# Attention scores as 32-row fp32r products in four row quarters, one ring of six PSUM banks for the scores and the feed-forward, and twice the low halves on GpSimd

## What is computed

```python
x = x + attn(layernorm(x))        # 16 heads of 8 columns, T = 512
#   qkv = x @ w_qkv + b_qkv
#   attn = softmax(where(causal, q @ k.T / sqrt(8), -inf)) @ v
#   out  = attn @ w_proj + b_proj
x = x + ffn(layernorm(x))         # d = 128, 8 experts, hidden 512
#   weights = p * (p > 0.5),  p = sigmoid(x @ Wg + bg)
#   h = relu(x @ W1[e] + b1[e]);  sum over e of weights[e] * (h @ W2[e] + b2[e])
```

## Time and profile before

| | |
|---|---|
| median of 3 runs | 763.07 us (762.34 to 765.86) |
| profiled execution, its own time | 762.58 us |
| its span | 760.8 us |
| PE / DVE / ACT / POOL busy | 723.6 / 528.3 / 407.4 / 276.2 us |
| mean granted clock of PE | 0.982 of full speed |
| PE's idle time before matmuls, from 106 us to 640 us | 534 us less 528.8 us busy |

### The profile page before, as it was taken

One profiled execution on the slowest core, in us unless ns is written; L12 is line 12 of the kernel. 1 busy time (PEld: TensorE's weight loads), 2 busy tenths in 40 slices (PEclk: granted clock), 3 DMA queues, 4 the chain that ended last, 5 costly groups with the idle time before them and its releaser, 6 DMA issues.

```text
span 760.8 us, 13160 instructions
## 1 busy us (share of the span) xinstructions
PE 723.6 (95%) x4515; PEld 413.8 (54%) x4515; DVE 528.3 (69%) x1044; ACT 407.4 (54%) x745; POOL 276.2 (36%) x424
## 2 busy tenths in 40 slices
PE   2969999999999999999999999999999999999996
PEld 2323345566555655555555645556455655567764
DVE  7977787678666786668865687666766676537543
ACT  1355665546555565556555655556545565654442
POOL 4173243334333343235422443333323433333232
PEclk9959999999999999999999999999999999999998
DMA  5521113110231122110221112111221101200300
GB/s 173 146 59 48 48 39 92 53 52 15 56 84 44 37 67 66 51 37 16 67 78 52 26 35 86 45 44 25 66 65 52 38 2 36 65 28 2 96 28 15
DMA packets 37698, 40.63 MB, mean 53 GB/s; under 512 B 5920, under 2 KB 26280, under 8 KB 37632
## 3 DMA queue, kind: packets, MB, share of 16 engines
q1 hardware_dynamic: 37104, 39.60, 18.9%
q10 hardware_dynamic: 528, 0.20, 0.2%
HBM read 23.52 MB, written 2.23 MB: 34 GB/s over the span
## 4 chain that ended last, share of the span: by engine, by line
PE 87%; DVE 4%; SPq 3%; issue 2%; ACT 2%; POOL 1%; DMA 0%; POOLq 0%; DVEq 0%; ACTq 0%
PE pv_bank L1160 11%; PE y_bank L1211 10%; PE z_bank L1026 10%; PE z_bank L1028 8%; PE y_bank L1215 8%; PE z_bank L1027 8%; PE y_bank L1213 8%; PE ring L1085 6%; PE ring L1082 6%; PE ring L1032 5%; PE ring L1098 5%; SPq L567 3%; PE ring L1139 1%; PE ring L1175 1%; PE ring L1026 1%
## 5 line engine op out<-in xcount | busy, mean ns | idle before, releaser
L794 ACT ACTIVATE h_hi<-z_bank 128x512 fp32r<-128x512 f32 x256 | 153.3, 599 | 186.3 <-PE z_bank L1028 159.9
L991 DVE SCALAR_TENSOR_TENSOR h_lo<-z_bank,h_hi 128x512 fp32r<-128x512 f32 x224 | 153.5, 686 | 86.7 <-ACT h_hi L794 85.4
L763 ACT ACTIVATE pt<-ring 128x512 f32<-128x512 f32 x292 | 163.9, 598 | 54.0 <-PE ring L1085 53.8
L941 DVE TENSOR_REDUCE negmax<-ring 128x1 f32<-128x512 f32 (+1 forms) x173 | 115.7, 683 | 43.3 <-PE ring L1098 43.1
L682 POOL TENSOR_SCALAR_AFFINE_SELECT pt<-pt 128x512 f32<-128x512 f32 x128 | 81.0, 645 | 153.5 <-ACT pt L763 153.2
L1211 PE MATMUL y_bank<-h_hi,w_lo 128*128 128x512 f32 x256 | 118.5, 463 | 2.4 <-POOL h_lo L689 1.8
L1026 PE MATMUL z_bank<-x2T_lo,w_hi 128*128 128x512 f32 x256 | 112.6, 440 | 0.2
L699 POOL TENSOR_TENSOR f_buf<-f_buf 128x512 f32<-128x512 f32 x56 | 71.9, 1284 | 107.9 <-DVE f_buf L1002 107.8
L1215 PE MATMUL y_bank<-h_lo,w_hi 128*128 128x512 f32 x256 | 101.1, 395 | 0.0
L1028 PE MATMUL z_bank<-x2T_hi,w_hi 128*128 128x512 f32 x256 | 101.0, 395 | 0.0
L1213 PE MATMUL y_bank<-h_hi,w_hi 128*128 128x512 f32 x256 | 100.6, 393 | 0.0
(11 more groups left out here) (171 smaller groups left out, 835.2 us busy)
## 6 DMA issues: line engine op xcount, KB each, us to landing
f_buf<-gates SPq DMA_DIRECT2D x64, 256.0 KB, 3.3
stack<-parts SPq DMA_DIRECT2D x192, 64.0 KB, 2.1
x_in<-in_L_attn_x SPq DMA_DIRECT2D x8, 256.0 KB, 3.1
pt<-in_L_ffn_W SPq DMA_DIRECT2D x1, 2048.0 KB, 10.0
out_x<-f_buf SPq DMA_DIRECT2D x8, 256.0 KB, 2.4
stack<-stack SPq DMA_DIRECT2D x32, 32.0 KB, 1.9
stack<-nmT SPq DMA_DIRECT2D x64, 6.0 KB
wqkv_in<-in_L_attn_w_qkv ACTq DMA_DIRECT2D x1, 192.0 KB, 3.2
```

What stands on the lines that cost most here:

```text
L763: sc.activation(pt[:, slot, :], b[:], ACT.Exp, scale=SCALE).then_inc(free_sem("ex", i, g, u), 1)
L794: sc.activation(h_hi[:, (i * SLOTS + s) % 3, :], z_bank[s % 2][:], ACT.Relu).then_inc(s_hhi, 1)
L941: v.tensor_reduce(dst, src, AX.X, ALU.max, negate=True).then_inc(free_sem("max", i, g, u), 1)
L991: v.scalar_tensor_tensor(out=h_lo[:, (i * SLOTS + s) % 3, :], in0=z_bank[s % 2][:], scalar=0.0, in1=h_hi[:, (i * SLOTS + s) % 3, :].bitcas ...
```

## The change

The scores' operands become two fp32r halves instead of three bf16 parts: three products of 8 rows and the maximum in two rows fit in 32 rows. Groups 0 and 2 lie in the upper 64 partitions, groups 1 and 3 in the lower 64, a head in a quarter. A call of both kinds, for two groups of different parity, then addresses all four quarters, and its matmuls are issued across the units, first pieces first. Part 1 and part 2 and their instructions go; SP makes 4 transfers for a group instead of 7, and one instead of two for the maxima. `nm` splits in two halves; its transposition becomes four fp32r matmuls with a stationary operand of 128 columns, of which 8 are filled. `z` takes a bank of the common ring, which has six instead of four. 8 of 32 low halves go through POOL, with a single `h_all`. The planner gets other costs, starts a ready `pv` ahead of a call of scores, and delays by two due units (`HALF_DUE`) a call that isn't of both kinds.

```diff
-Q_PART = (0, 0, 1, 0, 1, 2)
-K_PART = (0, 1, 0, 2, 1, 0)
-STACK_DMAS = 7
+Q_PART = (0, 0, 1)
+K_PART = (0, 1, 0)
+STACK_DMAS = 4
...
-RING = 4
-EARLY_RING = RING + 3
+RING = 6
+EARLY_RING = RING + 1
...
-POOL_SPLITS = [s for s in range(SLOTS) if s % 8 == 7]
+POOL_SPLITS = [s for s in range(SLOTS) if s % 4 == 3]
...
             due += SWITCH_DUE if form != "full" else 0
             if best is None or due < best[0]:
                 best = (due, key)
+        if pv and best and pv[0] + (PV_DUE if form == "full" else 0) < best[0]:
+            best = pv
+        if not best:
+            best = pv
         if pairs and free >= 2:
+            due = min(p[0] for p in pairs.values()) + (SWITCH_DUE if form == "full" else 0)
+            if free < 4 or len(pairs) == 1:
+                due += HALF_DUE
             if best is None or due < best[0]:
+                if pv and form == "full":
+                    start(now, "pe", pv[1])
+                    return
...
-        parts = sb("parts", [P, 6, T], BF16)
-        stack = sb("stack", [P, PAIRS, 2, T], BF16)
+        parts = sb("parts", [P, 4, T], F32R)
+        stack = sb("stack", [P, GROUPS // 2, 2, 2, T], F32R)
...
                 elif kind == "stack":
+                    rows = stack[64 * (g % 2):64 * (g % 2) + 64, g // 2].bitcast(F32)
                     for s, (a, b) in enumerate(zip(Q_PART, K_PART)):
+                        sp.dma_start(rows[s::4, :, :, :],
+                                     parts[32 * g:32 * g + 32, a:3 + b:2 + b - a, :].bitcast(F32)
+                                     ).then_inc(s_stack[g], 16)
...
-                elif kind in ("qpart", "kpart"):
-                    pool.wait_ge(*emptied(kind[0], i))
-                    g_.tensor_copy(parts[:, 3 * qk + 1, :], rest[:, qk, :]).then_inc(s_part1, 1)
...
+            def head_rows(g, j):
+                r = 64 * (g % 2) + 32 * (j % 2)
+                return stack[r:r + 32, g // 2, j // 2]
...
+                units = [(False, unit, max_pieces(unit, next_bank("max", *unit))) for unit in mx]
+                units += [(True, unit, exp_pieces(unit, next_bank("ex", *unit))) for unit in ex]
+                for k in range(2):
+                    for last_form, unit, pieces in units:
+                        if k >= len(pieces):
+                            continue
+                        out_, lhsT, rhs = pieces[k]
+                        stop = last_form and k == len(pieces) - 1
+                        last = mm(out_, lhsT, rhs, start=(k == 0), stop=stop, skip_group_check=True)
...
+                    for t in range(TB):
+                        last = mm(b[:, t * P:(t + 1) * P], nm[:, t, :], ident32[:], start=True, stop=True)
+                    last.then_inc(done, 1)
```

More of the change, by code:

```diff
@@ L61 @@
 PER_UNIT = SLOTS / UNITS_PER_SEQ
-SWITCH = 100
+UNIT_COST = 230
+ENTER = {"full": 190, "mask": 92, "scores": 190, "pv": 98}
 SWITCH_DUE = 0.3
-AFTER_PE, AFTER_OTHERS, AFTER_DMA = 170, 70, 2000
+PV_DUE = 0.3
+HALF_DUE = 2
+AFTER_PE, AFTER_OTHERS, AFTER_DMA = 175, 85, 2000
 def work_items():
@@ L239, in list_schedule @@
     emptier = {}
-    mode = "rows128"
+    form = "full"
     def at(time, what, key):
@@ L254, in start @@
     def start(now, engine, key):
-        nonlocal mode, banks
+        nonlocal form, banks
         cost = work[key][1]
@@ L260, in start @@
         if engine == "pe":
[L261 to L264, removed]
+            new = "pv" if item[0] == "pv" else "full"
+            if form != new:
+                cost += ENTER[new]
+            form = new
+            if item[0] not in ("y", "pv"):
                 fill(item)
@@ L273, in start_scores @@
     def start_scores(now, mx, ex):
[L274 to L285, removed]
+        nonlocal form
+        cost = ENTER["scores"] if form != "scores" else 0
+        form = "scores"
+        for unit in (*mx, *ex):
+            fill(unit)
+            ready["pe"].remove(("pe", unit))
+        cost += UNIT_COST * (2 if mx and ex and (mx[0][2] - ex[0][2]) % 2 == 0 else 1)
+        for unit in ex:
+            at(now + cost + AFTER_PE, "done", ("pe", unit))
         if mx:
-            mode = "rows128"
-            cost += SWITCH
+            form = "full"
+            cost += ENTER["mask"]
             for unit in mx:
-                cost += 80
+                cost += UNIT_COST // (4 if unit[3] < GH else 2)
                 at(now + cost + AFTER_PE, "done", ("pe", unit))
@@ L308, in pick_pe @@
                 continue
-            if item[0] not in ("z", "y", "pv") and not free:
+            if item[0] == "pv":
+                if pv is None or due < pv[0]:
+                    pv = (due, key)
+                continue
+            if item[0] != "y" and not free:
                 continue
@@ L443, in block_program @@
         pv_bank = bank("pv_bank")
-        z_bank = [bank("z_bank0"), bank("z_bank1")]
         y_bank = bank("y_bank")
-        ring += [*z_bank, y_bank]
+        ring.append(y_bank)
         s_ident = sem("s_ident")
@@ L1042, in max_pieces @@
                     for j in heads:
-                        rows = stack[64 * (j % 2):64 * (j % 2) + 64, (g * GH + j) // 2]
+                        rows = head_rows(g, j)
                         n = (q + 1) * P
@@ L1106, in _ @@
                     continue
-                if kind in ("z", "y", "pv"):
-                    pass
-                else:
+                if kind not in ("y", "pv"):
                     b = next_bank(*w)
```

199 lines of the change are left out of this document (87 added, 112 removed).

## The result

| | before | after |
|---|---|---|
| median of 4 runs each | 763.12 us (762.34 to 765.86) | 751.89 us (751.27 to 753.44) |
| profiled execution, its own time and its span | 762.58 us, 760.8 us | 752.44 us, 750.7 us |
| mean granted clock of PE | 0.982 | 0.960 |
| first z issued at | 108.12 us | 120.16 us |
| from the first z to the end | 652.7 us | 630.5 us |

The ratio is 0.985 (0.982 to 0.9879): 11 us faster, where 40 were forecast, and just outside the range of 700 to 750. The last two rows split it. From the first z on the kernel gained 22.2 us, with 32.6 forecast (terms 1, 2 and 4). Ahead of it, it lost 12.0 with 7 gained in the forecast: 19 of the missing 29 us. The same items lie ahead of the first z in both, but for one pair of ex units more in the changed kernel.

A forecast was written before the change was run, and what follows sets the result against it. PE was taken to bound the kernel from 106 to 640 us, the start to wait for data. 762.6 us with -35.6 - 3 - 7 + 2 + 4 = -39.6 gave 723 us, range 700 to 750.

The forecast's parts named there:

- Term 1: Calls of scores after the first z: joint calls stream in four quarters, 112.5 us instead of 148, so -35.6 us.
- Term 2: nm's transposition and pv on PE: nm between -6 and +6, taken as 0; pv ahead of calls -3 us.
- Term 4: New waits: y behind POOL's low halves +2 us (up to +26), four banks and common ring +4 (0 to +10).
- What bounds the kernel: PE bounds from 106 to 640 us, DVE has room up to 1.4; before that the start waits for data.
- I take 105 of 126: Number of calls after the first z that become joint, between 60 and 126; those ends give -10 and -47 us.
- pv's -3: A ready pv started ahead of a call of scores saves a border where it stood alone: -3 us, -9 at most.
- The +6: New waits after the first z: +2 us for y behind POOL, +4 for banks and the common ring.
- Term 3, the start: Ahead of the first z: fewer gather transfers and earlier last parts, partly given back by DVE: -7 us (0 to -12).
- The transfers: First sequence's gather on SP: 16 transfers instead of 28, 0.65 us each, so 7.8 us less.
- The calls ahead of the first z: Calls of scores before 106 us get cheaper, but PE waits for data there, so counted as 0.
- its own range: Whole time without rivals, 704 to 740 us, from joint calls (-47 to -25), start (0 to -12), waits (+3 to +14).

The follow-up runs named there:

- six early banks: The changed kernel, but y's bank not lent to the common ring before the first z (six banks there instead of seven): 748.85 us, ratio 0.9724.

## Why the prediction was off

**What bounds the kernel** was right from the first z on. PE sets the end, DVE has room, and PE's idle time didn't grow. For the start it was read from 20 to 60 us alone; from 60 to 108 us PE was busy for 44.97 of 48 us already before the change, and there it is PE's work and clock that count.

**Term 1, the mechanism: right.** The calls in the timeline above, and 786.4 us without joint calls, show that quarters stream together. The Trainium skill ("TensorE: Matmul & The Clock Gate", Part 3) says that row tiles overlap; the trace agrees, eight matmuls of 256 columns from 414.03 to 414.47.

**Term 1, the size: -26 instead of -35.6.** After the first z the planner's order has 81 calls in four quarters and 13 that share a half, where I took 105; 32 of max alone (21) and 38 of ex alone (29). Prices measured there: 0.77, 0.94, 0.73 (0.70 to 0.71 with units of one matmul, mostly 0.77 with two) and 0.63. Together 81 x 0.77 + 13 x 0.94 + 32 x 0.73 + 38 x 0.63 = 122 us, against 112.5 forecast and 148 before. The counts carry most of it: my 105, 21 and 29 at the measured prices make 114.5. The step that failed in this term is "I take 105 of 126". It had bounds (60 to 126), but no reading of when four banks are free and of which half the due groups are.

**Term 2.** nm went from 0.52 to 0.45, 32 times: -2 instead of 0. pv's -3 I can't separate.

**Term 4: no cost to be seen.** y waited 1.6 us behind POOL's 64 low halves (1.8 for 32 before); PE was idle for 1.9 of 510 us. The +6 wasn't there. That four low halves take 3.1 us less from the first z on may be a small cost of the eight; one profiled execution of each doesn't show it.

**From the first z on** these make -28, and the traces show -22.2. The prices are those of a call between two products of the full form. Calls next to pv or to another call share a border and cost less. That is argued; what the runs show is that counts times prices overstate: 5.6 us instead of 13 without the delay, 32 instead of some 40 with no joint calls. Part of the 6 us is the clock: it was at 0.50 from 369.2 to 372.6 and from 454.6 to 458.0 us, 3.4 us of lost clock that the kernel before didn't have there.

**Term 3, the start, is the step that failed most: -7 forecast, +12 measured.** Three things were wrong in it.

*The transfers.* Before the change the chain that ended last did run through SP, from 23 to 50 us:

```profile
23.01 0.71 SPq L567
...
28.92 6.09 SPq L567
...
47.32 0.59 SPq L567
47.96 1.82 DMA stack<-stack
```

Taking 13 us from it left other waits. In the run with six early banks the chain goes through DVE there, and 4.61 us of it are one layer norm's last step (`xn`), whose four instructions took 1.11 us before the change, at 38.75 us:

```profile
40.10 4.69 DVE L849 TENSOR_SCALAR xn<-x_in,mv,rstd 128x128 f32<-128x128 f32 x4
...
39.76 6.17 POOL L665 TENSOR_TENSOR w_lo<-f_buf,w_hi 128x512 fp32r<-128x512 f32 x5
```

It lies beside POOL's `w_lo`; that this is why it is slow is not shown.

*The calls ahead of the first z.* The prediction has them "cheaper too, but PE waits there: 0". Nearly all of them are single (54 of 58), and a single fp32r call is dearer by about 0.1. Two runs have the same items ahead of the first z and the full clock from 60 us on: the ring with bf16 parts, and six early banks in quarters. Up to their first z:

```profile
0.00:106.84 106.84, 80.21 (x550) 34.63 (x550) 85.09 (x185) 51.87 (x96) 45.14 (x84) 0.90 0.33 87
...
0.00:108.74 108.74, 85.93 (x551) 45.61 (x551) 83.16 (x181) 51.05 (x95) 39.13 (x67) 0.91 0.32 88
```

PE's idle time is 26.6 us with bf16 and 22.8 in quarters: so the quarters, with their shorter gather, bring 3.8 us there where the forecast had 7. PE's busy time is 5.7 us longer, and 58 single calls at about 0.1 are that. The two together are the 1.9 us by which the first z is later.

*The clock.* I read it as full from 106 us on and costed the start at it; that the change could alter it I didn't consider. From 60 to 108 us the mean is 0.73 where it was 0.96. Against six early banks, whose clock was full there, PE is busy for 10.1 us longer up to the first z, some 2 of them for a pair of max units, a pair of ex units and a pv more: about 8 us for the clock. If all of PE's time followed the clock, 48 us at 0.73 would be 35 at the full one and at 0.96 46: 11 us, an upper estimate. Shown: time goes with the clock within one program (17.1 us over 0.032; 16.6 us over 0.027), and in the profiled executions the loss lies ahead of the first z. From there to the end, the kernel with the old costs takes 758.6 - 130.7 = 627.9 us at 0.952 and six early banks 738.2 - 108.7 = 629.5 at 0.985.

**What stays open is why the clock falls.** Executions with bf16 scores were at 0.975 to 0.983, but for one of the kernel before, 966.92 us at 0.655; those with fp32r scores in quarters were at 0.948 to 0.989. The height of the matmuls isn't it (0.74 with 64 rows). Orders of the start gave 0.54, 0.73, 0.89 and 1.00 in the same stretch, but one execution each, and one program alone spreads nearly as far. Which property of that start decides, the operands' type among them, and why one program gets different clocks, no run here tells.

**The range.** The start was given 0 to -12, with no end on the side of a loss. With its +12 the time leaves 700 to 750, which the smaller term 1 alone (723 + 10) would not have done. And the upper ends of the terms themselves add up to 749, not to the 740 of "its own range".

**Where the gain came from.** By the profiled executions, with the joint calls after the first z:

| | joint calls | first z | first z to end |
|---|---|---|---|
| before | 12 | 108.12 us | 652.7 us |
| bf16, ring | 51 | 106.84 us | 642.1 us |
| bf16, ring, longer delay | 84 | 106.00 us | 635.3 us |
| the same, `SWITCH` 190 | 98 | 112.53 us | 627.7 us |
| the same, other streaming cost too | 95 | 112.05 us | 634.2 us |
| quarters without the ring | 55 | 120.04 us | 653.4 us |
| quarters, ring, no delay | 71 | 120.40 us | 636.1 us |
| the changed kernel | 94 | 120.16 us | 630.5 us |
| six early banks | 93 | 108.74 us | 629.5 us |
| old costs | 92 | 130.68 us | 627.9 us |
| old costs, six early banks | 85 | 110.88 us | 638.7 us |

From the first z on the time mostly follows the number of joint calls, and the ring, the delay and the planner's costs set that number. At a like number the quarters give little or nothing: with 92 to 94 joint calls they take 627.9 to 630.5 us, bf16 634.2 with 95 and 627.7 with 98; with 85 they take 638.7, bf16 635.3 with 84; and with 51 to 55 they are 11 us behind. A joint call saves 0.11 in quarters (0.88 to 0.77), a single one costs 0.10 (0.52 to 0.63 for ex, 0.66 to 0.77 for max units of two matmuls); with 94 joint and 70 single calls that is about even. What the dearer calls and the clock take at the start comes on top. The best median is the bf16 kernel's with the ring and the longer delay, 743.3 to 743.8 us; the only execution below 741 us is in quarters, 739.97 with six early banks at a clock of 0.985.

## What to carry to other kernels

When a change has several parts, price the one that lets the others happen first: here the shared ring with its delay, worth 12 us with the old operands, rather than the new form of the matmuls. Before a term is put at nothing because an engine waits, read the whole stretch: here PE waited up to 60 us and was busy for 94% of the next 48. A stretch in which the granted clock isn't full is not a fixed cost; forecast it as a range between its two levels, and compare versions over several executions with the clock beside each. Before taking a shorter transfer as a gain, look which engine is full beside it.

## What the runs showed of the hardware

The same program had a mean clock of 0.953 to 0.985 in four executions, and another 0.948 to 0.979 (three executions low, one high), worth 17 us each; in their profiled executions all low clock lies ahead of 110 us and in the last 4. PE can be fully busy at 0.50: 16.00 of 16.00 us from 90 to 106 us of the changed kernel. Entering the form of the quarters with fp32r weights costs 0.10 us more than entering that of the halves with bf16 (0.43 against 0.33 from an ex call's start to the next product). It is paid once for a call of up to eight matmuls in four quarters (0.44 to its masks), so their loads don't add up one behind the other.
